# Key-value products of two tiles moved into the norm ahead of the second mix, with the norm's turns on two single banks

## The reference, cut to what matters

```
m = jnp.mean(x, -1); v = jnp.var(x, -1)
xn = (x - m) / jnp.sqrt(v + 1e-5)                     # 3125 x 256
# L1 mix: 8 heads of 64
q, k, v = jnp.split(xn @ w_qkv.T, 3)                  # each 3125 x 512
k = instance_norm(k); v = instance_norm(v)            # over the 64 columns of a head
dots = einsum('bhnd,bhne->bhde', k, v)                # 8 matrices of 64 x 64, sums over all nodes
out = einsum('bhnd,bhde->bhne', q, dots) / N @ w_out.T + b_out
```

## Time and profile before

| | us |
|---|---|
| median of 3 runs | 2209.81 |
| lowest and highest | 2208.97, 2211.61 |
| profiled execution, its own time | 2207.67 |
| its span, first to last instruction | 2206.1 |
| TensorE busy in it | 2072.0 (94%) |
| VectorE busy | 1651.4 (75%) |
| ScalarE busy | 1238.5 (56%) |
| mean granted TensorE clock | 0.979 |

### The profile page before, as it was taken

The page is one execution under the profiler, slowest core; times in us unless marked ns, Lnnn a source line. Parts: engine busy times, 40 slices in busy tenths (PEclk is TensorE's granted clock), DMA queues, the critical chain, the costliest instruction groups (busy, mean ns, idle before and its releaser), DMA issues. The chain is left out here.

```text
span 2206.1 us, 46549 instructions
## 1 busy us (share of the span) xinstructions
PE 2072.0 (94%) x17896; PEld 1944.3 (88%) x17896; DVE 1651.4 (75%) x3102; ACT 1238.5 (56%) x2882; POOL 602.1 (27%) x462
## 2 busy tenths in 40 slices
PE   5759999999889999988999999999999999999996
PEld 3559999999779999987788999999989999999996
DVE  6998888885688888875657566666567868888885
ACT  5865555554547677665543444444443336767665
POOL 3100000000047777770000000000000016677775
PEclk9879999999989999999999999999999999999998
DMA  4434334335448777784004666466641026777876
GB/s 129 142 91 119 94 97 116 92 110 145 159 169 225 231 224 244 219 236 97 1 26 126 189 188 189 116 188 180 196 138 37 24 95 202 227 233 223 243 220 171
DMA packets 241111, 339.00 MB, mean 154 GB/s; under 512 B 33407, under 2 KB 202546, under 8 KB 240754
## 3 DMA queue, kind: packets, MB, share of 16 engines
q1 hardware_dynamic: 208908, 296.19, 42.7%
q0 software_dynamic: 28528, 35.76, 8.7%
q10 hardware_dynamic: 3446, 3.97, 0.6%
HBM read 258.89 MB, written 76.95 MB: 152 GB/s over the span
## 5 line engine op out<-in xcount | busy, mean ns | idle before, releaser
L2010 POOL DMA_INDIRECT SC<-xd,slot_i x128 | 191.4, 1495 | 789.4 <-DVE slot_q L1646 662.1
L2459 PE MATMUL bank<-WB_r,XN_r 128*128 128x448 f32 x1400 | 398.9, 366 | 0.4 <-DVE X L2252 0.4
L2413 DVE TENSOR_TENSOR WB_r<-WB,WB_r 128x448 fp32r<-128x448 f32 x350 | 219.2, 637 | 164.5 <-ACT WB_r L2408 164.5
L2408 ACT CAST WB_r<-WB 128x448 fp32r<-128x448 f32 x350 | 198.2, 568 | 244.8 <-PE bank L2459 242.7
L2459 PEld LDWEIGHTS bank<-WB_r,XN_r 128*128 128x128 f32 x1400 | 262.7, 188 | 22.8 <-DVE X L2252 0.8
L1940 PE MATMUL bank<-SC_r,WB_r 128*128 128x256 f32 (+1 forms) x2064 | 250.9, 281 | 8.3 <-issue 6.3
L1940 PEld LDWEIGHTS bank<-SC_r,WB_r 128*128 128x128 f32 x2064 | 244.3, 188 | 12.4 <-issue 11.9
L1060 ACT CAST WB_r<-bank 128x200 fp32r<-128x200 f32 x391 | 145.0, 371 | 159.4 <-PE bank L1043 158.6
L1955 PE MATMUL bank<-R_r,H_r 128*128 128x256 f32 x1752 | 213.4, 281 | 4.7 <-DVE R_r L1851 4.7
L1955 PEld LDWEIGHTS bank<-R_r,H_r 128*128 128x128 f32 x1752 | 207.2, 188 | 5.0 <-issue 5.0
L2400 POOL TENSOR_TENSOR WB<-WB,CB 128x128 f32<-128x128 f32 (+1 forms) x56 | 27.1, 486 | 593.9 <-DMA WB<-adjw 593.4
(11 more groups left out here) (461 smaller groups left out, 5135.7 us busy)
## 6 DMA issues: line engine op xcount, KB each, us to landing
WB<-adjw SPq DMA_DIRECT2D x350, 224.0 KB, 2.8
WB<-in_f_pack SPq DMA_DIRECT2D x127, 512.0 KB, 6.1
WB<-in_f_pack SPq DMA_DIRECT2D x62, 640.0 KB
adjw<-X SPq DMA_DIRECT2D x24, 1600.0 KB, 7.7
WB<-in_f_pack SPq DMA_DIRECT2D x65, 516.0 KB
xd<-XN SPq DMA_DIRECT2D x15, 640.0 KB, 5.5
y<-X SPq DMA_DIRECT2D x10, 640.0 KB, 3.3
X<-y SPq DMA_DIRECT2D x6, 640.0 KB, 7.0
```

The source lines that it names most:

```text
L2010: e.indirect_dma_start(yin[i % 2][:, q * D:(q + 1) * D], None, XD, bass.IndirectOffsetOnAxis(ap=slot_i[:, 2 * i + q:2 * i + q + 1], axis=0 ...
L2408: e.copy(split_w(m)[0], RAW[m % PR]).then_inc(S("whigh"), 1)
L2413: e.tensor_tensor(al, RAW[m % PR], ah.bitcast(F32), ALU.subtract).then_inc(S("wlow"), 1)
L2459: mm_ = e.matmul(conv_bank(k, band, c)[:, 0:PW], x[st][:, o], y, start=(st == 0 and i == 0), stop=(st == T - 1 and i == 2))
```

## The change

`turn_bank` gives the third norm (k = 2) one bank for each half, bank 3 for c = 0 and bank 6 for c = 1; the other norms keep their four. `turn_pe` there waits from g = 1 on for the copy of the group just before. The products of a tile become a function `keys_values_pe`. In the norm's loop TensorE runs it for tile 0 in pass g = 5 and for tile 1 in pass g = 6, in the place of the six constant matmuls, and the mix starts with tile 2. For that the first split moves on both engines from pass g = 6 to pass g = 4.

```diff
+    def turn_bank(k, g, c):
+        return B[(3, 6)[c]] if k == 2 else B[(2 * g + c) % 4]
+
     def turn_pe(e, k, g):
         ts = tiles_of(g)
         for c in range(2):
-            bk = B[(2 * g + c) % 4]
-            if g >= 2:
-                e.wait_ge(S(f"xt{c}"), G * k + g - 1)
+            bk = turn_bank(k, g, c)
+            deep = 1 if k == 2 else 2
+            if g >= deep:
+                e.wait_ge(S(f"xt{c}"), G * k + g - deep + 1)
...
             if ready is None:
-                warm_pe(e, 7, 6)
+                if g < 5:
+                    warm_pe(e, 7, 6)
+                else:
+                    keys_values_pe(e, g - 5)
...
+    EARLY = 2
+
+    def keys_values_pe(e, t):
+        if t == 0:
+            e.wait_ge(S("low1"), 2)
+        if t % 4 == 0:
+            e.wait_ge(S("low1"), 2 + 2 * (t // 4) + 2)
+        for c2, bk in enumerate((key_bank(t), value_bank(t))):
+            if c2 == 0 and t >= 4:
+                e.wait_ge(S("keys"), t - 3)
+            if c2 == 1 and t >= 3:
+                e.wait_ge(S("vals"), t - 2)
+            for c in range(2):
+                for n, (x, w) in enumerate(((xth, kvh), (xth, kvl), (xtl, kvh))):
+                    m = e.matmul(bk, x[:, c, t * 128:(t + 1) * 128], w[:, c, c2 * 512:(c2 + 1) * 512],
+                                 start=(c == 0 and n == 0), stop=(c == 1 and n == 2))
+            m.then_inc(S("kvm"), 1)
...
-        e.wait_ge(S("low1"), 0 + 2)
-        for t in range(T + 3):
+        for t in range(EARLY, T + 3):
...
-        norm_act(e, 2, lambda g: split_act(e, 0) if g == G - 1 else None)
+        norm_act(e, 2, lambda g: split_act(e, 0) if g == 4 else None)
...
-        norm_dve(e, 2, x_back(e), lambda g: split_dve(e, 0) if g == G - 1 else None)
+        norm_dve(e, 2, x_back(e), lambda g: split_dve(e, 0) if g == 4 else None)
```

More of the change, by code:

```diff
@@ L542, in turn_act @@
         e.wait_ge(S("xT"), 2 * (G * k + g) + 1)
-        e.copy(XT[:, 0, ts[0] * 128:(ts[-1] + 1) * 128], B[2 * g % 4][:, 0:len(ts) * 128]).then_inc(S("xt0"), 1)
+        e.copy(XT[:, 0, ts[0] * 128:(ts[-1] + 1) * 128], turn_bank(k, g, 0)[:, 0:len(ts) * 128]).then_inc(S("xt0"), 1)
         if g in BOTH.get(k, ()):
             e.wait_ge(S("xT"), 2 * (G * k + g) + 2)
-            e.copy(XT[:, 1, ts[0] * 128:(ts[-1] + 1) * 128], B[(2 * g + 1) % 4][:, 0:len(ts) * 128]).then_inc(S("xt1"), 1)
+            e.copy(XT[:, 1, ts[0] * 128:(ts[-1] + 1) * 128], turn_bank(k, g, 1)[:, 0:len(ts) * 128]).then_inc(S("xt1"), 1)
     def turn_dve(e, k, g):
@@ L552, in turn_dve @@
         e.wait_ge(S("xT"), 2 * (G * k + g) + 2)
-        e.tensor_copy(XT[:, 1, ts[0] * 128:(ts[-1] + 1) * 128], B[(2 * g + 1) % 4][:, 0:len(ts) * 128]).then_inc(S("xt1"), 1)
+        e.tensor_copy(XT[:, 1, ts[0] * 128:(ts[-1] + 1) * 128], turn_bank(k, g, 1)[:, 0:len(ts) * 128]).then_inc(S("xt1"), 1)
     def scores_pe(e, k, g):
@@ L2272, in mix1_pe @@
                 continue
[L2273 to L2284, removed]
+            keys_values_pe(e, t)
         for t in range(3, 5):
```

## The result

The changed kernel takes 2212.61 us (median of 16 runs, 2207.76 to 2216.03), the kernel before 2208.89 on the same chips (16 runs, 2205.78 to 2211.78): ratio 1.0016, 95% interval 1.001 to 1.0023 (2.2 to 5.1 us), so 3.7 us slower. Forecast were 4.0 us. The profiled execution has a span of 2211.1 us and takes 2212.54, 4.9 us more than that of before.

A forecast was written before the change was run, and what follows sets the result against it. It took ScalarE, with VectorE almost as full, to bound the norm and TensorE the mix. Later `dots` (2.5 us) plus clock (1.5) made 4.0 us on the median 2209.81, so 2213.8 us; range 2211.0 to 2217.0.

The forecast's parts named there:

- Steps 1 and 4: End of norm, TensorE's list: 5.67 us of products leave the mix, but with the late last turn 0.3 remains.
- Step 2: Third norm, single banks: VectorE's copy of a turn comes 0.75 us late, groups 3 and 4 come 0.67 late.
- Step 3: Pass 4: VectorE's split waits for ScalarE's copies, so statistics start at 1025.84 and group 5's normed tiles come 4.4 us late.
- Step 5: Start of the mix: first square at 1035.33 and `dots` of tile 0 at 1041.77, 2.51 us later than before.
- Step 6: TensorE's clock falls once, behind the 3.3 us wait ahead of `dots`, costing 1.5 us, from bounds of 0 and 3.4.
- what I had named as a sign: Expected in the profile: about 3.3 us of wait ahead of `dots` and a granted clock below 1.00 behind it.
- the rival of the second fall: Clock also falls in the stretch before tile 1, 1.6 us extra, sum 5.6, time 2215.4 us; chance 0.17.
- The faster case: Norm and split overlap, VectorE's stall is hidden, `dots` comes 4.3 us early, time 2205.5 us; chance 0.07.
- That the change does little: The split's stall and the shortened start-up cancel within 1 us, time 2210 us; chance 0.06.

The follow-up runs named there:

- e5: e3 with the products of tile 1 behind the last turn, two constant matmuls left ahead of `dots`; median -0.1 us against the kernel before (ratio 1.0).
- e1: The kernel before with only the third norm's single bank for each half; median +2.8 us against the kernel before (ratio 1.0009).
- e2: The kernel before with only the first split moved to pass 4 on both engines; median +4.6 us against the kernel before (ratio 1.0017).
- e10: e2 with 12 more constant matmuls in pass 5, in TensorE's wait; median +2.4 us against the kernel before (ratio 1.0007).
- e4: The changed kernel with two banks for each half again, constant matmuls into bank 0; median +3.2 us against the kernel before (ratio 1.0012).
- e3: The changed kernel with constant matmuls, 8 behind tile 0's products and 11 ahead of the first `dots`; median +2.7 us against the kernel before (ratio 1.0009).
- e8: e4 with constant matmuls, 6 ahead of tile 0's products and 11 ahead of the first `dots`; median -0.2 us against the kernel before (ratio 1.0).
- e6: The changed kernel with VectorE's first split in pass 5 and constant matmuls in both waits; median +2.1 us against the kernel before (ratio 1.0015).
- e9: e4 with VectorE's first split in pass 5, tile 0's products in pass 6, tile 1's behind the last turn, second split with tile 2; 2205.69 us against 2208.97 before.

## Why the prediction was right

- *Steps 1 and 4, TensorE's own list.* Right but for the clock. Products of tile 0 at 1026.14 (1025.98 forecast), the turn of group 5 at 1031.08 (1031.02). Then the turn took 1.6 us and not 0.96, and the products of tile 1 3.76 and not 2.80, so tile 2 began at 1037.27 and not 1035.6. e5 shows that tile 1's place ahead of the last turn costs 1.7 us, where I had 1.4 to 2.2.
- *Step 2, single banks.* Right: VectorE's copy of group 1's turn at 1015.34, 0.78 after where it stood; groups 3 and 4 0.73 and 0.74 late (the step says 0.67; its own s + 6.88 against s + 6.18 would be 0.70); and e1, +1.42 alone.
- *Step 3, the split in pass 4.* Right to 0.1 us: subtraction 1024.70 (1024.63), statistics 1025.91 (1025.84), square root 1027.83 (1027.75). e2 and e10 show it alone, 2.4 us where I had 1.9.
- *Step 5, the start-up chain.* 6.39 us from the first square to `dots` (6.44 forecast). The square itself came at 1036.89 and not 1035.33, and these 1.56 us are the low clock of the first stretch.
- *Step 6, the clock.* Here the number came out by luck. I put one fall of 1.5 us behind the wait ahead of `dots`. In the profile that wait came (2.97 us) and the clock held at 1.00, against what I had named as a sign. The fall came in the first stretch, behind a wait of 1.90 us, without one at `dots`, a case that my rivals do not have; it cost 1.6 us, the price that the rival of the second fall gives it. So the profile's 4.0 us and the forecast's 4.0 agree because 1.6 us at one place stood in for 1.5 at another. In e4 a wait of 2.98 us ahead of `dots` lost the clock and cost 2.85 us, not 1.5. On the median, e3 against the changed kernel gives 1.1 us, which the intervals do not resolve. The Trainium skill ("TensorE: Matmul & The Clock Gate", section "Why this matters for your kernels") warns that gaps between bursts cost clock. The traces agree where it fell behind 1.90 us (changed kernel), 3.38 (e2) and 2.98 (e4), and not at the 2.97 us of the changed kernel, the wait to which the forecast applied it. In the waits that e3, e8 and e10 fill, the clock is 1.00.
- *What step 6 left out.* It took from the earlier trace rows that the clock holds after 2.26 us between dense runs, from one execution; the last section shows the same place with both outcomes. And it looked for poor stretches only in passes 5 and 6, while the single banks also make TensorE wait in the norm, 1.62 us ahead of the turn of group 1 in the changed kernel. At that place the clock held in the profiles of e1, e5 and the changed kernel (1.50 to 1.75 us of wait) and fell in those of e3 and e6 (3.10 and 2.69), for 0.8 us each. In before and the versions with two banks a half the wait there is at most 1.00 us, and no turn of groups 1 to 4 runs at the low clock.
- *Rivals.* The faster case, a hidden stall, is out by the 1.78 and 2.64 us waits in the profile. That the change does little is out by the interval. Not shown is which part of the runs' spread (8.3 us between the changed kernel's fastest and slowest, 6.0 before) comes from this stretch.

The parts do not add: single banks 1.4 and early split 2.4 alone are 3.8, together with the tiles moved they are 2.4 to 2.5 without the clock. The products taken off TensorE's later list and the two banks ready for the first squares may give something back; no run separates this.

## What to carry to other kernels

Moving work of the busiest engine into a phase that another engine bounds gains only if nothing that the bounding engines wait for is queued behind it, on any list: here the moved products stood ahead of the last turn, and the step that prepares their operands ahead of the statistics. When two engines do a step in turn, put the second one's part where the first one's is already done, and look for free buffers before taking them from a running pipeline. The gain then came without taking out any result's work, by the order of the lists and the choice of banks (e9). And ask of each new wait of the busy engine what it does to the clock, also of the short ones that a missing second buffer makes: the forecast had the waits right to 0.1 us and the clock's place wrong.

## What the runs showed of the hardware

- Behind waits of TensorE of equal length, at the same place of the program, the clock held in one execution and fell in another. The clearest place lies ahead of every edit, so all twelve kernels have the same instructions there: the wait for VectorE ahead of line 1955 of the kernel before (rows of e1 and of the changed kernel, where the line has another number).

```profile
982.77 5.68 PE L1959 MATMUL bank<-R_r,H_r 128*128 128x256 f32 x48 [2.42 <-DVE R_r L1855]
983.11 7.42 PE L1962 MATMUL bank<-R_r,H_r 128*128 128x256 f32 x48 [2.42 <-DVE R_r L1858]
```

  Over the 5 us from each start the clock is 1.00 in e1 and 0.66 in the changed kernel, and the same 48 matmuls take 1.74 us more. Of the five profiles with a wait of 2.41 or 2.42 us there, two (e1, e4) kept the clock and three (changed kernel, e2, e3) lost it. The waits ahead of `dots`, 2.97 us in the changed kernel (1.00) and 2.98 in e4 (0.78 over 1035 to 1040, 0.54 over 1040 to 1045), look alike, but there the two kernels differ ahead of the wait too. A single profile thus doesn't give the price of a wait.
- A short wait can lose the clock every time. The 1.83 us wait of the fourth norm is in all twelve profiles, and all twelve lost the clock behind it, but for different times: from 1.7 us of full-speed work over the next 10 us (e1, e3, e9) to 3.4 (the changed kernel).
- Constant matmuls that are issued at half speed become a cost themselves: in e2 the turn of group 5 and the six constants behind it took 5.1 us (1030.11 to 1035.17), in e1 the same pair at full clock 2.3 (1027.28 to 1029.55).
